# Scatter matmuls of a routed feed-forward layer, split into two halves of 64 rows by 16 columns

## What is computed

```
h  = silu(x W_up^T + b_up) W_down^T + b_down          # 128 wide
q  = h W_q^T ; sim = q . keys                          # 8 heads, 45 keys, two halves
8 best keys of each half -> 64 sums -> 8 best experts per head   # 64 slots a token
z   = silu( (h . down_embed[indices]) * softmax(scores) )
out = sum over slots of z * up_embed[indices]          # 2048 experts, 256 wide
x   = x + tanh(g_ffn) * out
```

## Time and profile before

| | |
|---|---|
| median of 3 runs | 1285.93 us (1282.44 to 1288.79) |
| the profiled execution | 1286.89 us, span 1285.1 us |
| mean granted TensorE clock | 0.973 of 2.4 GHz |
| TensorE matmuls | 1181.4 us busy (92%), 19324 instructions |
| VectorE | 1122.3 us busy (87%) |
| ScalarE, GpSimd | 638.4 us (50%), 331.0 us (26%) |
| one steady turn | 36.6 us |

### The profile page before, as it was taken

One profiled execution on the slowest core, in us unless ns is written; L12 is line 12 of the kernel. 1 busy time (PEld: TensorE's weight loads), 2 busy tenths in 40 slices (PEclk: granted clock), 3 DMA queues, 4 the chain that ended last, 5 costly groups with the idle time before them and its releaser, 6 DMA issues.

```text
span 1285.1 us, 47501 instructions
## 1 busy us (share of the span) xinstructions
PE 1181.4 (92%) x19324; PEld 1042.7 (81%) x19324; DVE 1122.3 (87%) x4298; ACT 638.4 (50%) x1834; POOL 331.0 (26%) x152
## 2 busy tenths in 40 slices
PE   5676999999999999999999999999999999999866
PEld 3665888888888888888888888888888888888755
DVE  1457899999999999999999999999999999999963
ACT  3254465555545655555456555554565555545310
POOL 1223122333331223333311233332122333331110
PEclk9887999999999999999999999999999999999878
DMA  7005345554544465455444554554445545543562
GB/s 200 6 6 122 106 120 143 143 108 112 142 119 114 121 143 143 100 121 142 122 111 121 143 143 98 122 142 111 117 125 143 141 105 117 142 119 109 129 148 51
DMA packets 300320, 153.33 MB, mean 119 GB/s; under 512 B 278111, under 2 KB 291271, under 8 KB 291911
## 3 DMA queue, kind: packets, MB, share of 16 engines
q1 hardware_dynamic: 300103, 150.29, 47.3%
HBM read 78.44 MB, written 4.72 MB: 65 GB/s over the span
## 4 chain that ended last, share of the span: by engine, by line
PE 86%; DVE 6%; issue 5%; ACT 2%; POOL 1%; DMA 0%; SPq 0%; POOLq 0%; DVEq 0%; ACTq 0%
PE bank L989 16%; PE bank L833 12%; PE bank L820 11%; PE bank L870 9%; PE bank L843 8%; PE bank L939 5%; PE bank L878 3%; PE bank L910 3%; PE bank L858 3%; PE bank L920 3%; PE bank L889 2%; PE bank L976 2%; PE bank L907 2%; PE bank L956 1%; PE bank L853 1%
## 5 line engine op out<-in xcount | busy, mean ns | idle before, releaser
L989 PE MATMUL bank<-ue,coef 128*128 128x256 f32 x1024 | 226.5, 379 | 1.1 <-ACT coef L403 1.1
L340 POOL TENSOR_TENSOR rstd<-veps,minus_half 128x1 f32<-128x1 f32 x32 | 17.6, 551 | 783.4 <-DVE veps L736 783.4
L989 PEld LDWEIGHTS bank<-ue,coef 128*128 128x128 f32 x1024 | 192.1, 190 | 26.2 <-ACT coef L403 1.4
L833 PE MATMUL bank<-uc,hot_r 128*128 128x32 bf16 x6144 | 161.0, 177 | 32.8 <-issue 32.8
L833 PEld LDWEIGHTS bank<-uc,hot_r 128*128 128x128 bf16 x6144 | 157.5, 96 | 38.9 <-issue 38.8
L820 PEld LDWEIGHTS bank<-z,hot_rT 128*128 128x128 bf16 x2048 | 155.3, 96 | 29.3 <-issue 28.9
L820 PE MATMUL bank<-z,hot_rT 128*128 128x32 bf16 x2048 | 161.7, 177 | 7.4 <-DVE picked L571 5.9
L820 PE MATMUL bank<-zl,hot_rT 128*128 128x32 bf16 x2048 | 160.9, 177 | 0.0
L820 PE MATMUL bank<-zll,hot_rT 128*128 128x32 bf16 x2048 | 160.8, 177 | 0.0
L820 PEld LDWEIGHTS bank<-zl,hot_rT 128*128 128x128 bf16 x2048 | 155.9, 96 | 0.0
L820 PEld LDWEIGHTS bank<-zll,hot_rT 128*128 128x128 bf16 x2048 | 155.6, 96 | 0.0
(11 more groups left out here) (140 smaller groups left out, 2238.6 us busy)
## 6 DMA issues: line engine op xcount, KB each, us to landing
hot_rT<-expert_rows SPq DMA_DIRECT2D x64, 1024.0 KB, 6.4
xt<-in_x SPq DMA_DIRECT2D x32, 128.0 KB, 2.5
out<-x1k SPq DMA_DIRECT2D x32, 128.0 KB, 2.1
ue<-in_L_ffn_up_embed SPq DMA_DIRECT2D x1, 2048.0 KB, 17.1
ct<-in_ctx SPq DMA_DIRECT2D x32, 32.0 KB, 2.2
z<-in_L_ffn_W_up SPq DMA_DIRECT2D x1, 1024.0 KB, 8.5
expert_rows<-r_h SPq DMA_DIRECT2D x64, 8.0 KB, 1.8
hot_r<-hot_rT SPq DMA_TRANSPOSE x64, 7.0
```

Source lines behind the costliest of these rows:

```text
L833: last = mm(bG[k % 2][:, 32 * (q - 16 * k):32 * (q - 16 * k) + 32], hot_r[:, q, :], uc[:, n, q, :], start=(n == 0), stop=(n == 2))
L989: last = mm(bG0[:, 0:DM], coef[:, c, :, :].rearrange("r h q -> r (h q)"), ue[:, c, :], start=(c == 0), stop=(c == C - 1))
```

## The change

Each scatter matmul becomes two, of 64 rows and 16 columns. The first has the slots of the first token (partitions 0 to 63), the second those of the second token (64 to 127); each has the same 128 weights' columns and the lower or upper half of `hot_r`. The halves write different banks: first tokens to bG0 for pairs 0 to 31 and bP0 for pairs 32 to 63, second tokens to bG1 and bP1. `uc` loses its zero columns (and GpSimd's memset of it), so that one VectorE instruction of 128 partitions by 1024 writes a part where two of 64 by 1024 did. The four copies to `coef` stay four and of the same size, but the first two wait for step 1 and the last two for step 3. Step 2 waits for the copies of the similarities (they share bP), steps 1 and 3 for no other engine's reading of a bank.

```diff
-        uc = sb("uc", [128, 3, Q, 2 * C], H)
+        uc = sb("uc", [128, 3, Q, C], H)
...
-            step(nc.gpsimd.memset(uc[:, :, :, :], 0.0))
...
                 def coef_copy(k):
-                    Ct.wait(f"w_pe{k}")
+                    half, h = k // 2, k % 2
+                    Ct.wait(f"w_pe{2 * half + 1}")
                     if k == 0:
                         Ct.free("out_pe")
-                    copy(coef[:, :, :, 16 * k:16 * k + 16], bG[k % 2][:, :].rearrange("r (q h c) -> r c h q", q=16, h=2), f"w_sb{k}")
+                    copy(coef[:, :, h, 32 * half:32 * half + 32], (bG, bP)[half][h][:, :].rearrange("r (q c) -> r c q", q=32), f"w_sb{k}")
...
                     Ct.free("w_pe3")
-                    for half in range(2):
-                        rows = slice(64 * half, 64 * half + 64)
-                        last = nc.vector.tensor_tensor(uc[rows, n, :, C * half:C * half + C].rearrange("s q (c b) -> s q c b", b=2),
-                                                       hot_c[rows, :, :].rearrange("s q (c b) -> s q c b", b=2),
-                                                       u_h[rows, n, :, :].unsqueeze(2).to_broadcast([64, Q, C // 2, 2]), ALU.mult)
-                    last.then_inc(S[f"uc{n}"], 1)
+                    nc.vector.tensor_tensor(uc[:, n, :, :].rearrange("s q (c b) -> s q c b", b=2),
+                                            hot_c[:, :, :].rearrange("s q (c b) -> s q c b", b=2),
+                                            u_h[:, n, :, :].unsqueeze(2).to_broadcast([128, Q, C // 2, 2]), ALU.mult).then_inc(S[f"uc{n}"], 1)
...
                     Ct.wait_dma(f"hotr_in{k // 2}")
-                    Ct.wait(f"gm{k + 2}" if k < 2 else f"w_sb{k - 2}")
+                    if k == 0:
+                        Ct.wait("zs3")
+                    elif k == 2 and Fw:
+                        Fw.wait("sim_sb0")
+                        Fw.wait("sim_sb1")
+                    elif k == 2:
+                        pe.wait_ge(S["sim_sb0"], TILES)
+                        pe.wait_ge(S["sim_sb1"], TILES)
                     for q in range(16 * k, 16 * k + 16):
                         for n in range(3):
-                            last = mm(bG[k % 2][:, 32 * (q - 16 * k):32 * (q - 16 * k) + 32], hot_r[:, q, :], uc[:, n, q, :],
-                                      start=(n == 0), stop=(n == 2))
+                            for h in range(2):
+                                rows = slice(64 * h, 64 * h + 64)
+                                last = mm((bG, bP)[k // 2][h][:, 16 * (q % 32):16 * (q % 32) + 16], hot_r[rows, q, :], uc[rows, n, q, :],
+                                          start=(n == 0), stop=(n == 2))
```

## The result

The changed kernel takes 1450.67 us (median of 4 runs, 1447.03 to 1453.85), the kernel before 1284.83 us in the same comparison: ratio 1.1284, 95% interval 1.125 to 1.1319. The profiled execution took 1447.03 us, its span is 1445.3 us.

What follows compares the result with a forecast made beforehand. TensorE's chain was taken to bound the turn, VectorE barely releasing the scatter. Per turn 3.85 - 0.50 + 0.10 + 2.05 = 5.50 us, 159.5 in 29; 1286.9 + 159.5 + 7, less 1, gives 1452 us; range 1375 to 1490.

Steps and rivals of the forecast that it cites:

- The bound and the wait for `uc`: Ahead of each scatter: shorter VectorE work on `uc` ends TensorE's wait of 0.43 us; -0.50 us a turn.
- The halves overlap: In the scatter: two half matmuls run side by side, 25 ns a pair, 4.80 us of stream as before.
- C: In the scatter: the halves do not overlap, 9.6 us, net +4.85 us a turn, 1436 us; chance 0.15.
- D: In the scatter: half-height weights load in 112 ns instead of 25, 21.5 us a scatter, some 1800 us; chance 0.04.
- Fetch: In the scatter: each instruction block takes 3.6 us to fetch, so the scatter lasts 8.8 us; +3.85 us a turn.
- Rival B: At block borders in the scatter: fetch keeps up and the halves overlap, so faster, 1266 us; chance 0.10.
- The clock: Dense matmuls behind each scatter: streaming and standing in turn leaves half clock for about 4.1 us; +2.05 us a turn.
- Rival A: In and behind the scatter: fetch-bound, but the clock stays up, 1391 us; chance 0.18.
- The sum: Whole kernel: 5.50 us a steady turn, 159.5 us in 29 turns, +7 us at the end; 1452 us.
- the tail: Last three tiles: scatter +2.9 us each, `uc` -2.1 each, tiling +0.1, copies 1.2 in all, clock about 1.0 each; +7.
- Copies and memset: Copies to `coef` cost nothing in steady turns, 0.6 us in each of the last two tiles; the starting memset counts zero.

Runs made afterwards that it cites:

- with GpSimd: The kernel before the change with two of its six coefficient instructions moved from VectorE to GpSimd: 1345.69 us, ratio 1.0474.

## Why the prediction was right, and where it was not

**The bound and the wait for `uc`: right.** The 0.43 us ahead of the scatter went with the shorter `uc`, in the changed kernel and in the run with half of `uc` alone, and came back with six instructions. The first start of the scatter follows the last of `dense(2)` by 0.21 us, forecast 0.20.

**The halves overlap: right.** 25 ns a pair of halves, as taken from the attention's tiles; the two starts of a pair are 3 to 4 ns apart, forecast 7. The Trainium skill's rule ("TensorEngine Tiling (Array Packing)", Instruction Overhead), by which a matmul takes as long with one column as with 60, agrees with this trace for one and the same tile (25 ns each in the run without overlap, with 16 columns or 32). Two row tiles have that price side by side, so it did not make two halves cost twice one whole. Rivals C and D fall.

**Fetch: right in mechanism and size.** Scatter forecast at 8.8 us, measured 8.7 (forecast bounds 7.3 and 9.4, measured 6.5 to 10.3: the spread was too narrow). Stops of 2 us were forecast ahead of each of three blocks; mostly there are two a scatter, and the first border passes with a short stop or none. Packets 3.9 us apart in the view above, 3.5 elsewhere. That the block holds 256 instructions is shown by the 127 or 128 matmuls between stops, and that it is fetch and not the tiles by the scatter of half the pairs and by the full-size stream issued twice. The Trainium skill ("Runtime: NRT & Kernel Launch", Instruction fetch mechanics) has the size of the page right; "mostly hidden" is what the runs contradict: at 12.5 ns an instruction the fetch just shows (stops of a few tenths), at 6.25 ns it is the bound (8.7 us for 4.8 us of stream). Rival B falls.

**The clock: right in size, too narrow in cause.** Outside the scatter the turn has 33.5 us, where 31.8 - 0.5 + 0.1 = 31.4 were due: 2.1 us against the 2.05 forecast. The weak step is the sentence that leads there: that it is the streaming and standing in turn that brings the clock down, so that a stream without stops would keep it. Stops can do it, as the runs with half of the pairs and with GpSimd show. But they are not needed: in a stream of 10 us without long stops the clock falls with 16 columns or with 64 rows, and stays up with 128 rows and 32 columns. The changed kernel has both the stops and the small matmuls, and which of the two brings its clock down was not separated. That the size came out right is in part luck: the time outside the scatter is the same with the stops (33.5 us) as without them (33.6 us with the halves one after the other). The evidence at hand, a stretch of 1.66 us busy followed by half clock, showed a pause among full-size matmuls, and could say nothing on small ones. Rival A, whose clock stays up, falls with the granted clock of 0.91 from 150 to 1200 us. The narrow cause did cost three expectations: 1400 for 1482, 1435 for 1494, and, with the tiling, 1330 for 1450.

**The sum.** 28 turns of 5.50 us were forecast and are 5.50. The first scatter comes 7.5 us earlier (forecast 0, and not shown to be the change's doing). From the 29th scatter to the end are 123.0 us (1445.3 - 1322.3) against 109.5 before, 13.5 more, where one turn and the tail came to 5.5 + 7. In the tail the prediction gives no working for its +2.9 us a scatter; the last three took 2.9, 3.0 and 5.4 us more. The total for the profiled execution was forecast at 1453 and is 1447.0: 6 us off, nearly all of it at the start. That the median of 1450.67 lies within 1.4 us of the forecast 1452 is luck of the draw: the profiled execution is the fastest of the four.

**Copies and memset: right.** No wait for `coef` in steady turns; the memset is worth some 1 us, less than the starts of the same stream differ by.

## What to carry to other kernels

Count instructions, not only array time: a stream that uses up 256 TensorE instructions (128 matmuls with their loads) in less than about 3.6 us is bound by their fetch, and splitting matmuls to save columns or rows doubles what has to be fetched. In this kernel a wait that was filled by reordering, while another engine was tenths behind, only moved; less work on that engine is what paid. And a long stream of small matmuls, or one with stops in it, had a price behind it, in the clock of the dense matmuls that follow, so read the granted clock there too.

## What the runs showed of the hardware that was not expected

- TensorE's clock fell to half in streams of 128 rows by 16 columns and of 64 rows by 32 columns at 25 ns a matmul without a pause, and not in one of 128 by 32: 0.89, 0.89 and 1.00 of full speed from 150 to 1200 us. The first differs from the last in nothing but the columns moved, and took 71 us more.
- With the same 192 small matmuls a turn, the clock fell in all 11 turns in which fetch stops drew the scatter out to 3.3 us or more, and in 1 of the 17 in which they ran through in 2.4 or 2.5 us.
- Matmuls on the two row halves of the array start 3 to 4 ns apart; on one and the same half, 25 ns, with 16 columns or with 32.
- A cast on VectorE took 1.85 us beside a GpSimd instruction of 1.93 us, and 0.23 us alone.
